# Gates copied later in three layers, half of the key copies and the first queries moved around the seam of layer 0 and its attention

## What is computed

```python
# attention of layer 1 (_L1_xattn): queries from the normed x, keys and values from the context
q = rope((layernorm(x) @ wq.T + bq).reshape(b, s, 16, 8))
k = rope((ctx @ wk.T + bk).reshape(b, s, 16, 8))
attn = softmax(q @ k.T / sqrt(8))
x = x + tanh(g_xattn[1]) * ((attn @ v) @ wo.T + bo)

# a mixture of experts (_L0_ffn; layers 1 and 3 differ in activation and routing)
gates = layernorm(x) @ gate_w.T + gate_b          # 1024 tokens, 8 experts
w = softmax(top2(gates))                          # zero for the experts that are not chosen
for e in range(8):
    h = gelu(xn @ w1[e] + b1[e])                  # 128 -> 512
    out = out + w[:, e] * (h @ w2[e] + b2[e])     # 512 -> 128
x = x + tanh(g_ffn[0]) * out
```

## Time and profile before

| what | value |
|---|---|
| median of 3 runs | 605.32 us (602.43 to 605.65) |
| the profiled execution | 602.64 us, of which 600.9 us span |
| PE, busy share of the span | 94% |
| DVE | 74% |
| ACT | 69% |
| POOL | 17% |
| granted PE clock, mean | 0.994 |
| chain that ended last | PE 70%, DVE 13%, ACT 12% |

### The profile page before, as it was taken

One profiled execution on the slowest core, in us unless ns is written; L12 is line 12 of the kernel. 1 busy time (PEld: TensorE's weight loads), 2 busy tenths in 40 slices (PEclk: granted clock), 3 DMA queues, 4 the chain that ended last, 5 costly groups with the idle time before them and its releaser, 6 DMA issues.

```text
span 600.9 us, 8811 instructions
## 1 busy us (share of the span) xinstructions
PE 565.9 (94%) x3304; PEld 392.2 (65%) x3304; DVE 447.4 (74%) x696; ACT 414.2 (69%) x579; POOL 104.0 (17%) x69
## 2 busy tenths in 40 slices
PE   7999999989999999999897989999998998999997
PEld 5667887856777777775231337466546776788886
DVE  4367987878658899887989875766677836887786
ACT  4779899936756556657999965434514856988885
POOL 5400000011210000003989813100000310000000
PEclk9999999999999999999998999999998999999999
DMA  6208120200200812020000026306410100802000
GB/s 237 65 11 314 36 70 1 75 2 2 75 1 4 316 42 71 2 70 1 5 2 1 1 71 181 102 2 196 120 36 1 53 21 2 314 36 71 35 1 35
DMA packets 16782, 40.27 MB, mean 67 GB/s; under 512 B 1834, under 2 KB 6058, under 8 KB 16740
## 3 DMA queue, kind: packets, MB, share of 16 engines
q1 hardware_dynamic: 16740, 39.71, 19.8%
HBM read 39.01 MB, written 0.70 MB: 66 GB/s over the span
## 4 chain that ended last, share of the span: by engine, by line
PE 70%; DVE 13%; ACT 12%; issue 4%; POOL 1%; ACTq 0%; DVEq 0%; POOLq 0%
PE ps L712 38%; ACT work L1093 6%; PE ps L755 4%; DVE h_lo L1606 3%; PE ps L452 3%; PE ps L738 2%; PE ps L584 2%; PE ps L469 2%; PE ps L740 2%; PE ps L739 2%; PE ps L555 2%; PE ps L569 2%; PE ps L459 2%; PE ps L694 1%; PE ps L446 1%
## 5 line engine op out<-in xcount | busy, mean ns | idle before, releaser
L1606 DVE TENSOR_TENSOR h_lo<-h_act,h_hi 128x512 fp32r<-128x512 f32 (+1 forms) x136 | 118.3, 874 | 41.9 <-ACT h_hi L1138 41.2
L712 PE MATMUL ps<-n_hi,w_hi 128*128 128x512 f32 (+1 forms) x232 | 85.9, 404 | 4.7 <-ACT h_act L1124 1.8
L1138 ACT CAST h_hi<-h_act 128x1024 fp32r<-128x1024 f32 (+1 forms) x88 | 75.3, 856 | 13.3 <-PE ps L712 11.0
L712 PE MATMUL ps<-n_hi,w_lo 128*128 128x512 f32 (+1 forms) x232 | 83.1, 392 | 0.0
L712 PE MATMUL ps<-n_lo,w_hi 128*128 128x512 f32 (+1 forms) x232 | 83.0, 391 | 0.0
L1814 POOL TENSOR_TENSOR rstd<-var_eps,minus_half 128x4 f32<-128x4 f32 x16 | 17.8, 1113 | 317.4 <-DVE var_eps L1270 317.4
L712 PE MATMUL ps<-h_hi,w_hi 128*128 128x512 f32 (+1 forms) x184 | 65.6, 399 | 2.6 <-DVE h_lo L1606 2.6
L712 PE MATMUL ps<-h_hi,w_lo 128*128 128x512 f32 (+1 forms) x184 | 64.1, 391 | 0.0
L712 PE MATMUL ps<-h_lo,w_hi 128*128 128x512 f32 (+1 forms) x184 | 64.0, 390 | 0.0
L1093 ACT ACTIVATE work<-work,p_rest 128x2048 f32<-128x2048 f32 x31 | 59.4, 1996 | 0.4 <-DVE work L1466 0.4
L1131 ACT ACTIVATE h_act<-ps 128x512 f32<-128x512 f32 (+1 forms) x48 | 28.6, 596 | 39.1 <-PE ps L712 39.1
(11 more groups left out here) (234 smaller groups left out, 1020.4 us busy)
## 6 DMA issues: line engine op xcount, KB each, us to landing
work<-g_rows SPq DMA_DIRECT2D x36, 512.0 KB, 6.4
w_f<-in_w SPq DMA_DIRECT2D x20, 512.0 KB, 3.6
w_f<-in_w SPq DMA_DIRECT2D x8, 544.0 KB, 3.6
work<-in_w SPq DMA_DIRECT2D x2, 512.0 KB, 4.4
work<-g_rows SPq DMA_DIRECT2D x4, 256.0 KB, 9.4
p_rest<-in_p_rest SPq DMA_DIRECT2D x1, 714.0 KB, 9.9
p_attn<-in_p_attn SPq DMA_DIRECT2D x1, 546.5 KB, 6.9
x<-in_xT SPq DMA_DIRECT2D x1, 512.0 KB, 3.6
```

The source lines that it names most:

```text
L712: mm = pe.matmul(dst[i], wap(wt, e, lo, size, rows), mv[i], start=(first and c == 0), stop=(last and c == 2))
L1138: act.copy(places(h_hi, m, step), places(h_act, m, step)).then_inc(s["hi"], 1)
L1606: dve.tensor_tensor(lo, src, hi.bitcast(F32), ALU.subtract).then_inc(s["lo"], 1)
```

## The change

Three things are moved, and the work itself stays the same but for six bf16 products of `keep_busy`.

1. In the expert layers 0, 1 and 3, ACT copies the gates after step 8 (before: step 6 in the plain layers, 7 in layer 1), and DVE calls `between` once more, ahead of the last part of the routing.
2. Four of the eight `expand_keys` (the second half's) leave the steps 25 to 30 and stand on ACT behind layer 0; the other four go from steps 17, 19, 21, 23 to 17, 20, 23, 26.
3. In layer 0, PE's norm of the first half moves from the steps 37, 38, 41 to 36, 37, 39, and `queries(0, 0)` goes to step 41, ahead of the last two down products. DVE's `finish(6, 1)` goes behind `norm_out(2, 0)`, and `query_rows(0, 0)` ahead of `finish(7, 1)`. Attention 0 opens with `scores(0, 0)` and `scores(0, 1)` around the second half's norm, with `keep_busy` ahead and between, and DVE takes `soft(0)` and `soft(1)` ahead of `norm_out(2, 1)`.

```diff
@@ attention(i) on PE
                 if i == 0:
-                    queries(0, 0)
+                    keep_busy(4, 4)
+                    scores(0, 0)
                     norm_mean(2, 1)
+                    scores(0, 1)
                     norm_var(2, 1)
-                    scores(0, 0)
+                    keep_busy(2, 4)
                     norm_spread(2, 1)
-                    scores(0, 1)
@@ PE
-            moe(MOES[0], {37: [lambda: norm_mean(2, 0)], 38: [lambda: norm_var(2, 0)], 41: [lambda: norm_spread(2, 0)]})
+            moe(MOES[0], {36: [lambda: norm_mean(2, 0)], 37: [lambda: norm_var(2, 0)], 39: [lambda: norm_spread(2, 0)], 41: [lambda: queries(0, 0)]})
@@ attention(i) on ACT
+                if i == 0:
+                    query_rows(0, 0)
                 norm_square((2, 6)[i], 1)
                 norm_copy((2, 6)[i], 1)
-                if i == 0:
-                    query_rows(0, 0)
@@ moe on ACT
-                    if step == (7 if m.gated else 6):
+                    if step == 8:
                         copy_gates()
@@ ACT
-            heads = {step: [lambda t=t, h=h: expand_keys(0, t, h)] for t, steps in enumerate(((17, 19, 21, 23), (25, 27, 28, 30))) for h, step in enumerate(steps)}
+            heads = {step: [lambda h=h: expand_keys(0, 0, h)] for h, step in enumerate((17, 20, 23, 26))}
             moe(MOES[0], {**heads, 41: [lambda: norm_square(2, 0)], 42: [lambda: norm_copy(2, 0)], 43: [lambda: load_table(ACT.Exp)]})
+            for h in range(4):
+                expand_keys(0, 1, h)
             attention(0)
@@ attention(i) on DVE
                 if i == 0:
-                    query_rows(0, 0)
+                    soft(0)
                     norm_eps(2, 1)
-                    soft(0)
+                    soft(1)
                     norm_out(2, 1)
-                    soft(1)
@@ weigh_chosen on DVE
                 if L != 2:
+                    between()
                     below = route_view("lg", E)
@@ DVE
                           35: [lambda: finish(MOES[0], 6, 0)], 38: [lambda: finish(MOES[0], 7, 0)], 41: [lambda: norm_eps(2, 0)],
-                          42: [lambda: finish(MOES[0], 6, 1)], 43: [lambda: norm_out(2, 0), lambda: finish(MOES[0], 7, 1)]})
+                          43: [lambda: norm_out(2, 0), lambda: finish(MOES[0], 6, 1), lambda: query_rows(0, 0), lambda: finish(MOES[0], 7, 1)]})
```

## The result

| | before | after |
|---|---|---|
| median of 8 runs each, us | 605.35 (602.43 to 606.28) | 600.83 (599.39 to 601.89) |
| profiled execution, us (span) | 602.64 (600.9) | 601.89 (600.1) |

The changed kernel takes 0.9943 of the time of before, with a 95% interval of 0.9921 to 0.9966: by this ratio it is faster by 3.5 us, between 2.1 and 4.8; the medians differ by 4.5. The two profiled executions differ by 0.75 us only: that of the changed kernel is the slowest of its eight runs, that of before (602.64) lies near the fastest of the kernel before (602.43). Most lines of the changed kernel stand 1 to 3 lower than in the rows of before.

The account below looks back on a forecast made before the run. PE, busy 94% of the span, was taken as the bound. Layer 0 -2.7, seam +1.6, layer 1 +0.25 and layer 3 -2.9 sum to -3.75 us: 598.9 profiled, 601.5 as median, range 597.5 to 605.5.

Parts of the forecast that it names:

- the forecast's case: Whole kernel: all waits of the openings go, seam +1.6; -3.75 us, by its bounds -2 to -5; chance 0.52.
- Layer 0's opening, -2.7: Layer 0's gates: PE's three waits of 0.21, 0.97 and 0.69 us all go, -2.7 us, at least -1.2.
- The 0.27 per wait: PE: the first product after a wait takes 0.50 us instead of 0.228, so 0.27 us on top of each wait.
- Layer 3's opening, -2.9: Layer 3's gates: three waits go, a new one of 0.5 for rt_w comes; -2.9 us, between -1.2 and -3.4.
- Layer 1, +0.25: Layer 1's gates: PE's transposes wait 0.3 to 0.65 for rt_w, a 0.18 wait goes; +0.25 us, between 0 and +0.5.
- Key copies, 0.7 at step 32: Layer 0, step 32: with fewer key copies ACT is about 0.7 us earlier, counted in the seam.
- The seam, +1.6 with the 0.7 of the keys in it: Layer 0's end to attention 0: `soft(2)` comes at 141.4 for 139.80, +1.6 us, bounded by 0 and +3.2.
- The second mean is late because `finish(7, 1)` is behind the query rows: Attention 0's opening: the second mean waits for `finish(7, 1)` on DVE and starts at 130.7, 4.3 us later.
- The clock as full in attention 0's opening: Attention 0's opening: clock assumed full in the forecast, since four more warm products stand ahead.
- The 1.3 us that the prediction put down for a fall in attention 1's opening: Attention 1's opening: a clock fall was taken to cost 1.3 of the 3.2 us by which it exceeds attention 0's.
- The rival: Attention 0's opening: the clock falls there as in attention 1's; -2.4 us in all, 602.9 us, chance 0.22.

Follow-up runs that it names:

- the call: Only the additional call of `between` in DVE's gate weights, layers 0, 1 and 3, on the kernel before: 605.39 us, ratio 1.0010.
- gates and keys: The changed kernel without its third part, so gates in all three layers and key copies, seam as before: 598.27 us, ratio 0.9922.
- only the new order of attention 0's opening: Gates and keys plus only the order in which attention 0 opens, `finish(7, 1)` staying ahead of the query rows: 601.12 us, ratio 0.9954.
- all three kernels that took one piece of the third part on gates and keys: Gates and keys plus only attention 0's new order (601.12 us), only the earlier norm and queries (606.40), or only the earlier norm (601.12).
- the copy alone: Only the gates' copy moved to step 8 in layers 0, 1 and 3, on the kernel before: 600.13 us, ratio 0.9938.
- the 72 later runs: The kernel before, unchanged, run 72 times more beside the experiments: 600.8 to 607.4 us, depending on the averaged granted clock.
- gates (layers 0 and 3) and keys: Kernel before with gates changed in layers 0 and 3 alone and key copies behind the layer; layer 1 and seam as before: 597.69 us, 0.9890.
- the added products: Gates (layers 0 and 3) and keys plus unused PE products in the pair sums and ahead of attention 1's spread: 595.81 us, 0.9853.

## Why the prediction was right, step by step

The forecast was 601.5 us (597.5 to 605.5), the median is 600.83. It was the forecast's case that came true: the waits of the openings go, and the seam costs. The terms, as the runs show them (times of the changed trace put back into those of the old one by adding 0.68 for the start and 2.81 for layer 0's opening):

- *Layer 0's opening, -2.7*: measured -2.81. All three waits went, and the copy of 1.00 us lies beside PE's work. The 0.27 per wait on top of its idle time held.
- *Layer 3's opening, -2.9*: measured -3.0, with a new wait of 0.39 for the 0.5 expected.
- *Layer 1, +0.25*: measured +0.29, with a wait of 0.61 at the transposes (0.3 to 0.65 expected). It is the difference of two larger terms, +0.78 for the call and -0.56 for the copy.
- *Key copies, 0.7 at step 32*: measured 0.7, in the wait and in `soft(2)`.
- *The seam, +1.6 with the 0.7 of the keys in it*: this term was mis-sized. Without the keys it is 3.07 us (the changed kernel against gates and keys), so +2.3 with them. The earlier mean and variance wait 0.23 and 1.26, foretold were 0.3 and 1.4, and the variance starts at 118.40 as worked out. But the queries start at 124.87 for 124.67, the first scores at 129.92 for 129.6, and from there to `soft(2)` it takes 12.12 us for 11.8, since mean, scores and variance take 3.17 us (127.54 to 130.71) where 2.9 were put down for them: 0.2, 0.1 and 0.3, so that `soft(2)` stands at 142.04 for 141.4.
- *The second mean is late because `finish(7, 1)` is behind the query rows*: this step failed as a cause, though its number was about right. With `finish(7, 1)` early the opening is no faster (only the new order of attention 0's opening, above). The mean is late because it stands on PE behind scores that wait for the query rows. In the changed kernel x is ready at 127.49 and the scores end at 127.5, so that DVE's order cost nothing there; the number came out because the two ends fall together, which is luck.
- *The clock as full in attention 0's opening*: held in the trace of the changed kernel, with its windows from 120 to 165 us at 1.00, and the eight turns run there at full clock: 1.04 us for the eight transposes of `turn(0)`, where they take 1.92 at the low clock of the kernel with only the new opening. (Attention 0 begins in the ninth slice of the earlier trace rows, which the prediction leaves out; it shows 9 too.) The 1.3 us that the prediction put down for a fall in attention 1's opening are 1.5: from its first scores to `soft(2)` it takes 13.39 us with a stretch and 11.91 in the traces without. The rival is no fancy, though: the clock fell there in all three kernels that took one piece of the third part on gates and keys, and in one that kept the old seam (the copy alone).

The terms add up to -2.8 - 3.0 + 0.3 - 0.7 + 3.1 = -3.1 us. The profiled executions differ by 0.75 = 0.7 (start) + 3.1 - 3.2 (clock in the pair sums) + 0.15 that is left over. Over all runs the ratio gives 3.5 us, and its interval (2.1 to 4.8) holds the 3.1. The medians differ by 4.5 since that of before, 605.35, falls among its slower runs; in the 72 later runs the medians of the same kernel are 603.9 to 604.6. At equal mean clock the changed kernel is faster by about 2.6 us at 0.994 and 3.6 at 0.991, if its runs are held against those 72. So the forecast gained about 0.6 us too much at the seam, and that the median of the changed kernel lies below 601.5 all the same is the luck of the medians.

## What to carry to other kernels

An instruction that waits on an in-order engine costs what stands ready behind it, so put that work ahead of it; both lines that won here do only this. An operation put earlier gains only if its inputs are early too: the mean and the variance, moved by one step, met waits of 0.23 and 1.26 us that they hadn't had. And split a change into its parts: this one is a gain of 6 us and a loss of 3, and inside its gain layer 1 is again a gain of 0.6 and a loss of 0.8.

## What the hardware showed that was not expected

Where PE is paced by another engine, its clock is at risk although each single wait is short. Timeline of gates (layers 0 and 3) and keys, PE, in the pair sums:

```profile
319.27 1.07 PE L694 MATMUL ps<-work,p_rest 128*32 128x512 f32 x8 [1.33 <-ACT work L1093]
321.17 1.07 PE L694 MATMUL ps<-work,p_rest 128*32 128x512 f32 x8 [0.83 <-ACT work L1093]
...
325.26 1.07 PE L694 MATMUL ps<-work,p_rest 128*32 128x512 f32 x8 [1.13 <-ACT work L1093]
```

No wait is longer than 1.33 us, and behind them, as in all thirteen traces without the added products (the lowest windows at 0.66 to 0.82 between 320 and 345 us), the clock is at 1.2 instead of 2.4 GHz for part of the next windows (0.75, where 1.00 is 2.4 GHz). The low clock hurts later than where it is earned: it costs nothing while ACT sets the pace (168.07 us before, with windows at 0.88 and 0.78) and 3.2 us when PE is the bound again (171.29). The Trainium skill ("TensorE: Matmul & The Clock Gate", A second HAM failure mode: psum-queue depth-cycling) tells of a kernel whose clock swings because PE idles briefly and often between groups of products; these rows agree with it. Three unused bf16 products in each wait, 0.8 us of PE's idle time, together with the longer `keep_busy` in attention 1, held the mean granted clock of all six runs at 0.997 or above, and these drew together to 2 us where they had spread over 3 without them.
